# A two-layer attention and expert kernel: first stage unrolled, routing constants moved, 1 KB row pieces

## What is computed

```python
xn = layernorm(x)
s  = attention_16_heads_of_8(xn, rope)                      # layer 0, left branch
g  = silu(ffn0(xn))                                         # layer 0, right branch
x  = x + s * g
xn = layernorm(x)
s  = delta_rule_attention(xn)                               # layer 1, left branch
g  = silu(sinkhorn_top2_experts(xn))                        # layer 1, right branch
x  = x + s * g
# ffn0: r = rmsnorm(xn) * gamma1; r = attention_16_heads_of_64(r) + o_b + r
#       an = rmsnorm(r) * gamma2; top 3 of 31 experts by softmax(an @ router_w + router_b)
#       out = shared_expert(an) + gated sum of the 3 experts' outputs + an + r
```

## Time and profile before

| | |
|---|---|
| median of three runs | 3122.18 us (3119.8 to 3138.54) |
| the profiled execution | 3139.03 us, span 3137.3 us |
| mean granted TensorE clock | 0.799 |
| PE busy | 2254.3 us, 72% |
| DVE busy | 1810.1 us, 58% |
| ACT busy | 1169.5 us, 37% |
| POOL busy | 1004.4 us, 32% |

### The profile page before, as it was taken

One profiled execution on the slowest core, in us unless ns is written; L12 is line 12 of the kernel. 1 busy time (PEld: TensorE's weight loads), 2 busy tenths in 40 slices (PEclk: granted clock), 3 DMA queues, 4 the chain that ended last, 5 costly groups with the idle time before them and its releaser, 6 DMA issues. The chain is left out here.

```text
span 3137.3 us, 44896 instructions
## 1 busy us (share of the span) xinstructions
PE 2254.3 (72%) x15735; PEld 1476.4 (47%) x15735; DVE 1810.1 (58%) x3632; ACT 1169.5 (37%) x2599; POOL 1004.4 (32%) x1222
## 2 busy tenths in 40 slices
PE   2328888799999999985537631576987774767991
PEld 1114444355555555553325521444876662446881
DVE  4338888566667666653524323596936666972333
ACT  2215666465556555552201112342011114542330
POOL 1341221055555555551552256100000002772330
PEclk8668999899999999996558865677557676778996
DMA  2121211421444120004015533234341101214553
GB/s 58 60 64 38 42 33 31 155 96 56 152 138 138 55 98 5 1 1 79 35 44 161 169 95 84 58 89 120 100 120 41 41 21 33 49 33 163 185 170 87
DMA packets 231724, 251.05 MB, mean 80 GB/s; under 512 B 63062, under 2 KB 212346, under 8 KB 230170
## 3 DMA queue, kind: packets, MB, share of 16 engines
q1 hardware_dynamic: 208634, 211.95, 23.4%
q0 software_dynamic: 14432, 32.17, 3.3%
q10 hardware_dynamic: 8448, 4.20, 0.5%
HBM read 193.03 MB, written 125.41 MB: 102 GB/s over the span
## 5 line engine op out<-in xcount | busy, mean ns | idle before, releaser
L953 ACT ACTIVATE a_p<-a_s_ps,a_nmax 128x512 f32<-128x512 f32 (+3 forms) x512 | 266.8, 546 | 99.3 <-DVE a_nmax L867 99.3
L867 DVE TENSOR_REDUCE a_nmax<-a_s_ps 128x2 f32<-128x1024 f32 (+3 forms) x256 | 204.9, 821 | 138.9 <-PE a_s_ps L768 134.1
L925 POOL TENSOR_SCALAR a_p<-a_p,a_rden 128x512 f32<-128x512 f32 (+3 forms) x512 | 262.6, 532 | 13.1 <-DVE a_rden L874 13.1
L558 DVE TENSOR_REDUCE a_shift<-a_s_ps 128x2 f32<-128x1024 f32 (+3 forms) x256 | 202.2, 820 | 53.9 <-PE a_s_ps L465 51.8
L964 ACT COPY a_e<-a_pt_ps 128x1024 f32<-128x1024 f32 (+3 forms) x256 | 174.5, 713 | 110.3 <-PE a_pt_ps L781 110.3
L623 ACT ACTIVATE a_e<-a_s_ps 128x1024 f32<-128x1024 f32 (+1 forms) x192 | 166.0, 884 | 109.3 <-PE a_s_ps L465 109.1
L781 PEld LDWEIGHTS a_pt_ps<-ident,a_p 128*128 128x128 f32 x1280 | 146.7, 141 | 126.8 <-issue 66.8
L763 PE MATMUL a_s_ps<-a_kT,a_qT 64*128 64x512 f32 (+3 forms) x1024 | 192.4, 472 | 6.9 <-ACT a_p L953 2.2
L781 PE MATMUL a_pt_ps<-ident,a_p 128*128 128x128 f32 x1280 | 173.1, 274 | 17.3 <-ACT a_e L964 17.3
L795 PE MATMUL a_y_ps<-a_e,a_v 128*64 128x512 f32 (+3 forms) x1024 | 155.6, 447 | 9.6 <-DVE acc L886 4.7
L2805 DVE TENSOR_TENSOR f_act<-f_silu,f_gu 128x256 f32<-128x256 f32 x156 | 65.7, 421 | 167.7 <-ACT f_silu L2784 167.0
(11 more groups left out here) (479 smaller groups left out, 5344.9 us busy)
## 6 DMA issues: line engine op xcount, KB each, us to landing
f_w<-in_wgud SPq DMA_DIRECT2D x39, 768.0 KB
l_band<-in_fir_long SPq DMA_DIRECT2D x16, 768.0 KB
x_w<-in_w SPq DMA_DIRECT2D x78, 128.5 KB
x_xr<-x_d SPq DMA_DIRECT2D x78, 128.0 KB
y_d<-x_yr POOLq DMA_DIRECT2D x78, 128.0 KB, 2.5
parts_d<-p_parts SPq DMA_DIRECT2D x16, 384.0 KB, 2.5
a_qs<-parts_d SPq DMA_DIRECT2D x96, 64.0 KB
a_ks<-parts_d SPq DMA_DIRECT2D x96, 64.0 KB
```

Of the source, the lines that this page charges most:

```text
L558: last = nc.vector.tensor_reduce(shift[n % 2][:, i, :], bank_of("q", g)[:, :, c:c + (i + 1) * P], AX.X, ALU.max, negate=True)
L867: last = nc.vector.tensor_reduce(nmax[g % 4][:, 2 * at:2 * at + 2], s_ps[g % 2][:, :, c:c + width(i)], AX.X, ALU.max, negate=True)
L925: last = nc.gpsimd.tensor_scalar(piece, piece, rden[g % 4][:, 2 * at + h:2 * at + h + 1], 1.0, ALU.mult, ALU.mult)
L953: last = nc.scalar.activation(p[g % 4][:, h, c:c + width(i)], s_ps[g % 2][:, h, c:c + width(i)], ACT.Exp, bias=nmax[g % 4][:, col], accum_ ...
```

## The change

In `prepare` the hardware loops are written out. Each of the 8 input loads has a buffer and a semaphore of its own and is issued at the start; constants come in four groups, each with its own semaphore, waited for where first needed; `xn`, `xnT`, `xfT` have two buffers, `parts` four. ScalarE's list of a round becomes: copy `xnT`, squares, root, first casts of the round before, the next round's root, second casts, copies of `xf` and v. GpSimd's six operations of a round go by kind instead of by half. VectorE does the next round's statistics between; tables and masks are computed in rounds 1, 2, 3, 5, the sines at the end. `v0` is set to 1.0 only in its last column.

In `attn1` SP issues the ten constants of `route`, the copy of `fill` and the `ids`, behind the second input load; `route` has no SP part and no wait for constants. In `route` TensorE makes the next round's logits ahead of this round's counts, ScalarE turns the next round before copying the gates, and VectorE adds the shared expert's output one round later.

Rows of a tile in `experts0` (load and store) and `experts1` (load) are dealt two neighbours to a partition, so that a piece of a DMA is 1 KB and not 512 B. `join0` has four buffers `yg` instead of two.

```diff
@@ prepare, ScalarE
-            roots(0)
-            copies(0)
-            with a.Fori(1, B) as b:
-                roots(b)
-                split(b - 1)
-                copies(b)
-            split(B - 1)
+            root(0)
+            for b in range(B):
+                turned(b)
+                squares(b)
+                rms_root(b)
+                if b:
+                    high(b - 1)
+                if b + 1 < B:
+                    root(b + 1)
+                if b:
+                    mid(b - 1)
+                values(b)
+            high(B - 1)
+            mid(B - 1)
+            tables()
@@ prepare, VectorE
-            norm(0, 0)
-            with v.Fori(0, B // 2 - 1) as i:
-                for s in range(2):
-                    norm(i * 2 + (s + 1), 1 - s)
-                    products(i * 2 + s)
+            spread(0)
+            nc.vector.memset(st["v0"][:, :, :, D0:D0 + 1], 1.0)
+            for b in range(B):
+                normed(b)
+                if b + 1 < B:
+                    spread(b + 1)
...
+                mean_square(b)
+                scaled(b)
+                products(b)
@@ attn1, SyncE
             load_x(1)
+            for dst, src in ((rc["gamma"][:, :], d["gamma2"].partition_broadcast(P)), (rc["wr"][:, :], d["router_w"]),
...
+                sp.dma_start(dst, src).then_inc(route_in, 16)
+            sp.dma_start(d["sorted"], d["fill"]).then_inc(filled, 16)
+            sp.dma_start(d["hs"][:, :, P:P + 1], d["ids"], allow_slow_non_contiguous=True).then_inc(filled, 16)
@@ route, VectorE
             for b in range(rounds):
                 logits(b)
                 if b + 1 < rounds:
                     normed(b + 1)
+                if b:
+                    shared(b - 1)
                 choose(b)
                 place(b)
-                shared(b)
+            shared(rounds - 1)
             plan()
@@ route, TensorE
+            turn(0)
+            logits(0)
+            for b in range(rounds):
                 for i in range(2):
                     after(pe, h_ready, 2 * b + i)
                     nc.tensor.matmul(sh_ps[:, :], ws[:, 0:P], anT[:, i, :], start=True, stop=True).then_inc(sh_done, 1)
                 if b + 1 < rounds:
                     turn(b + 1)
+                    logits(b + 1)
                 pe.wait_ge(both_ready, b + 1)
@@ experts0
-                sp.dma_start(xr[j % R][:, :, :], d["x0"][bass.ds(r, TILE0), :].rearrange("(i p) c -> p i c", p=P))\
+                sp.dma_start(xr[j % R][:, :, :], d["x0"][bass.ds(r, TILE0), :].rearrange("(p i) c -> p i c", p=P))\
@@ join0, GpSimd
-                after(gp, f_ready, b - 1)
+                after(gp, f_ready, b - Y + 1)
```

More of the change, by code:

```diff
@@ L171, in store @@
                 for i in range(2):
+                    n = 2 * (b % 2) + i
                     sp.wait_ge(low_ready, 2 * b + i + 1)
[L173 to L178, removed]
-                for s in range(2):
[L180 to L187, removed]
+                    sp.dma_start(d["parts"][i, b, :, :, :].rearrange("t p s -> p t s"), parts[n][:, :, :])\
+                        .then_inc(stored[n], 16)
+            for i in range(4):
+                sp.wait_ge(stored[i], 16 * (B // 2))
+            for i in range(2):
+                sp.wait_ge(xfT_stored[i], 16 * (B // 2))
         @block.vector
@@ L1191, in root, with turned @@
                 nc.scalar.activation(rms[:, :], ms[:, :], ACT.Sqrt).then_inc(rms_ready, 1)
-            squares(0)
-            root(0)
-            for b in range(rounds):
+            def turned(b):
                 a.wait_ge(anT_done, b + 1)
+                after(a, lg_done, b)
                 after(a, sh_done, 2 * b)
@@ L1200, in _ @@
                 last.then_inc(anT_ready, 1)
-                if b + 1 < rounds:
-                    squares(b + 1)
+            squares(0)
+            root(0)
+            turned(0)
+            squares(1)
+            for b in range(rounds):
                 a.wait_ge(lg_ready, b + 1)
@@ L1210, in _ @@
                     nc.scalar.activation(hsh[:, i, :], sh_ps[:, :], ACT.Gelu, bias=ws[:, 2 * P:2 * P + 1]).then_inc(h_ready, 1)
+                if b + 1 < rounds:
+                    turned(b + 1)
+                if b + 2 < rounds:
+                    squares(b + 2)
                 a.wait_ge(gT_done, b + 1)
@@ L1226, in turn, with logits @@
                 last.then_inc(anT_done, 1)
-            turn(0)
-            for b in range(rounds):
+            def logits(b):
                 pe.wait_ge(anT_ready, b + 1)
@@ L1407, in join0 @@
         wo = sb("wo", [P, P])
[L1408 removed]
+        Y = 4
+        yg = [sb(f"yg{i}", [P, NB, TOPK, P]) for i in range(Y)]
         xs = [sb(f"xs{i}", [P, NB, P]) for i in range(2)]
```

298 lines of the change are left out of this document (159 added, 139 removed).

## The result

The changed kernel takes 3024.64 us (median of four runs, 3021.76 to 3027.04), 0.9655 of the kernel before (95% interval 0.9634 to 0.9676; before on the same chip 3130.36 us). Its profiled execution has a span of 3025.3 us against 3137.3, 112.0 us less; I had forecast 155 and 2967 us, with a range that ended at 3015. The direction held and the size didn't. (The 2967 was counted from 3122.18 us; with one more run the median of the kernel before is 3130.36, so 8.2 of the 57.6 us by which 2967 was missed are this base.) Since the stages don't overlap, the difference splits exactly.

What follows compares the result with a forecast made beforehand. The stages don't overlap; the first stage's round was taken as a chain, not a load. Gains of 111.6 (first stage), 10.4 and 23 (routing), 2 (1 KB pieces) and 8 (join) sum to 155: from 3122.2 to 2967 us, range 2920 to 3015.

Steps and rivals of the forecast that it cites:

- With four buffers the 16.6 us go; what is late next is VectorE: Join stage: GpSimd's 16.6 us of waiting for a buffer vanish; gain taken as 8 us, between 16.6 and -10.
- 10.4 forecast: Routing stage, start: with no constants to wait for, 10.4 us are gained.
- 33.9 forecast: Routing rounds: 33.9 us each instead of 41.6, with 3.5 for late waits; gain 23 us, ends 0 and 34.
- slots 31 to 36 us apart: Routing stage: a sign that would show the prediction right; slots 40 us apart would show it wrong.
- The 24 scatters behind the last slot stay; `plan` is beside them: End of the routing stage: the last burst of scatters stays as before; no loss was counted there.
- (E): Rival: ScalarE's order isn't what holds the first stage's round, so only the other 44 us are gained: 3078; chance 0.03.
- the collisions: First-stage round: VectorE operations meeting GpSimd cost 1.0 us more each; two of four places taken, a round of 11.6 us.
- (A): Rival: GpSimd is in VectorE's way everywhere, first-stage round 13.6 us; gain 141 us, so 2981; chance 0.14.
- 2 us forecast: Expert stage: SP issues loads of 1 KB pieces faster, 78 x 0.027 = 2 us gained, between 0 and 3.
- the 5 MB: Second attention: 5.03 MB of added loads cost 0; 32 us if all came on the path.
- (B): Rival: late waits grow with unbroken indirect DMAs; routing rounds keep 41.6 us, the join gains nothing: 2998; chance 0.18.
- (D): Rival, slower: in routing VectorE's dependent steps each go on 4.0 us late; 3360 at 90 steps; chance 0.06.

Runs made afterwards that it cites:

- the old order, run again: The changed kernel with the old order of work in the routing stage, constants still loaded in the second attention: 3031.14 us, the stage 196.5 us.
- the experiment with narrow differences: The changed kernel with GpSimd's four differences of a first-stage round cut from 128x512 to 128x8: 3005.81 us, the stage 99.2 us.

## Why the prediction was wrong

The step that failed is the last of the change part by part, the join stage: "With four buffers the 16.6 us go; what is late next is VectorE". I had named the cause and the row, and priced it wrongly: I gave a loss of at most 10 us and took a gain of 8, because I read the late waits as single events. They are a state, and the trace of before had it: the row of 1895.49 is the fourth of six late steps behind the 28th gather (5.7, 4.6, 2.1, 4.0, 4.5 and 5.1 us), 55 us into the gathers and not 35. From there on nearly all such steps of VectorE are 2 to 6 us late until GpSimd stands still for several us. The two gaps of 8.8 and 7.9 us were what ended that state in the kernel before; I booked them as waste. Taking them away cost 17.6 us, and two buffers bring it back: 3007.58.

**Routing.** The start was right (10.4 forecast; the first slot comes 10.6 us sooner). The rounds were right in their mean (33.9 forecast, 34.0 measured) by luck: I had added 3.5 us of late waits to each; in the first two VectorE waited 9.2 and 8.6 us for counts that TensorE had ended 10.0 and 4.9 us before, and in the last, which is shorter anyway, for none. By my own sign, slots 31 to 36 us apart, no round passed. What failed for the sum is "The 24 scatters behind the last slot stay; `plan` is beside them". The last slot came 25.9 us after the third, while a burst takes 30.4, so it waited 5.4 us for the third burst to end; and the sum of the shared expert, behind which `plan` stands, came 27.3 us after TensorE, so that the stage ended 19.5 us behind the last scatter and not 10.2 as before. That is 14.6 of the 23 us given back; the old order, run again, shows both halves of it.

**First stage.** ScalarE's order did hold a part of the round, against (E), but the copy's place is only a third of what a round lost; the prediction put nearly the whole round down to it, and no run tells which of the other edits gave the 7.5 us. (Between 29.6 and 217.2 us lie seven rounds and a tail of 31 us, not eight rounds; the sum used seven. The operation beside the row of 1.17 us is GpSimd's difference L280, which writes bf16.) The mis-sized term is the collisions: I took two of four places at 1.0 us each; three were hit, with 0.98, 1.80 and 0.84 us, 3.6 in all. (A), which had all four, gave 13.6 against the measured 12.8; seven rounds took 89.4 us where I had 83.2 with the tables. The rule of the Trainium skill (SBUF — State Buffer, SBUF: two separate sides) that speaks of VectorE forms with two SBUF inputs next to a reading GpSimd was right for `xf` and `acc`: no row of before could show it, and the experiment with narrow differences does (2.94 and 1.53 us fall to 1.14 and 0.69).

**1 KB pieces.** 2 us forecast. SP's issuing fell by more: it takes 182.6 to 184.1 us in the three kernels with 512 B pieces and 175.5 to 179.8 in those with 1 KB. The drain, which I had at nothing, takes 4.6 of it back, and the run shows no difference. The stage is 5.9 us shorter than before, but it takes 196.1 and 198.5 us in two kernels with the old code, so what is left isn't told from the spread.

**The attentions** took the constants and the 5 MB without a wait: -1.0 us.

**The rivals.** (B) was nearest for the whole, at 2998, though it let the join gain nothing and didn't see a loss. (D) had the right picture, some 4 us a step in a state that lasts, and the wrong stage. I had put it in routing, where VectorE's own steps stayed on time (below) and updates of TensorE were late. The range's upper end, 3015, let both stages gain nothing; that one of them could lose stood in (D) alone, outside it.

## What to carry to other kernels

A wait can be worth its time. Before a buffer is added to remove GpSimd's pauses, look at what the other engines do in the longest unbroken row of indirect DMAs: if their dependent steps are late there, the pauses may be what lets them catch up, as they were here. And a step that is moved sooner can end up waiting behind a burst that used to be over; follow the last piece of work of the stage, not only its rounds.

## What the runs showed of the chip

In the join and the routing stage semaphore updates came up to 27 us late while GpSimd issued indirect DMAs without a pause. With gathers this starts behind the 28th to the 31st, and sooner behind an earlier pause; with scatters TensorE's updates were late from about the 20th of the first burst. Half the bytes or half the rows leave it as it is. TensorE's late updates came 2.8, 3.5 and 6.0 us after the end of a burst in the changed kernel. (TensorE's ends are modelled in the trace, so its lateness is less certain than VectorE's.) In the join stage VectorE's own steps were late; in the routing stage they were not, with TensorE's turned gates, ready at 1461.6, reaching ScalarE at 1470.44:

```profile
1461.13 0.46 DVE L1160 TENSOR_TENSOR r_eq<-r_z,hot 128x248 f32<-128x248 f32 x1
1461.62 0.41 DVE L1161 TENSOR_REDUCE slotf<-r_eq 128x8 f32<-128x248 f32 x1
1470.44 1.05 ACT L1256 COPY r_gT<-r_gT_ps 32x512 f32<-32x512 f32 x2 [17.37 <-DMA a_xT<-xfT_d]
```

Why one kind is late here and another there I could not tell. Every time here is that of an execution with a recorded span; whether updates are late in one that isn't recorded, no run shows. And GpSimd's drain behind 78 stores took 6.42 to 6.52 us with pieces of 1 KB and 1.78 with 512 B, in every run, also not explained.
